# A DLRM tower on one core: a wait for the last group's landing ahead of each group of four gathers

## What is computed

```python
e = jnp.stack([tbl_0[ids[:, 0]], ..., tbl_26[ids[:, 26]]], axis=1)   # (2048, 27, 128)
dot = jnp.einsum('bnd,bmd->bnm', e, e)       # 27 x 27 products of each sample
z = dot.reshape(2048, 27 * 27)[:, idx]       # the 351 pairs i < j
h = jnp.concatenate([z, dense_ctx], axis=1)  # 367 features
h = jnp.maximum(h @ W_top1 + b_top1, 0.0)    # 512
h = jnp.maximum(h @ W_top2 + b_top2, 0.0)    # 256
y = h @ W_top3                               # (2048, 1)
```

## Time and profile before

| | us |
|---|---|
| time, median of 3 runs | 709.78 (707.19 to 711.47) |
| profiled execution, time | 705.33 |
| profiled execution, span from first to last instruction | 703.5 |
| TensorE matmuls busy | 407.6 |
| GpSimd busy | 246.3 |
| VectorE busy | 272.8 |
| ScalarE busy | 142.0 |

### The profile page before, as it was taken

How to read it: one execution, slowest core, us unless ns; L and a number is a source line. 1 busy time by engine, 2 the same in 40 slices (tenths; PEclk the granted TensorE clock), 3 DMA queues, 4 the chain that set the end, 5 groups by cost and what they waited for, 6 DMA issues and landing times.

```text
span 703.5 us, 15274 instructions
## 1 busy us (share of the span) xinstructions
PE 407.6 (58%) x6218; PEld 360.3 (51%) x6218; DVE 272.8 (39%) x804; ACT 142.0 (20%) x189; POOL 246.3 (35%) x264
## 2 busy tenths in 40 slices
PE   3327501892529724497245945179552892639875
PEld 3316401891429723396235935069441791529854
DVE  6506222781308603185032833028421581308211
ACT  3307210140103301023011321002210240103421
POOL 6750457007440347103561064600546007440000
PEclk9759755796759957599576976659766896759997
DMA  7921512011111211102111111110211111110000
GB/s 211 263 61 39 153 42 69 19 56 54 33 35 32 75 37 45 48 4 73 42 46 46 44 52 30 48 34 18 76 31 49 36 53 54 30 36 2 2 2 1
DMA packets 22295, 36.58 MB, mean 52 GB/s; under 512 B 12662, under 2 KB 13310, under 8 KB 22252
## 3 DMA queue, kind: packets, MB, share of 16 engines
q1 hardware_dynamic: 13996, 19.01, 9.3%
q0 software_dynamic: 8256, 16.92, 8.5%
HBM read 35.90 MB, written 0.01 MB: 51 GB/s over the span
## 4 chain that ended last, share of the span: by engine, by line
PE 52%; issue 32%; another core or an unknown queue 7%; DVE 3%; DMA 2%; ACT 2%; SPq 1%; DVEq 0%; ACTq 0%
PE emb_ps L670 20%; PE gram_ps L714 13%; PE mlp_ps L733 5%; PE emb_ps L706 4%; PE mlp_ps L747 3%; DMA embT<-in_tbl 2%; PE emb_ps L686 2%; DVE onehot L564 1%; PE mlp_ps L776 1%; PE mlp_ps L755 1%; PE mlp_ps L724 1%; SPq L271 1%; PE mlp_ps L781 1%; ACT onehot L425 0%
## 5 line engine op out<-in xcount | busy, mean ns | idle before, releaser
L391 POOL DMA_INDIRECT rows<-in_tbl,idx x256 | 244.0, 953 | 378.4 <-PE emb_ps L706 256.7
L714 PE MATMUL gram_ps<-embT 128*32 128x26 f32 x4096 | 97.0, 220 | 235.1 <-issue 214.6
L564 DVE TENSOR_SCALAR onehot<-ids_b,row_of 128x256 fp32r<-128x256 int32 x694 | 193.5, 356 | 44.9 <-PE emb_ps L670 37.5
L714 PEld LDWEIGHTS gram_ps<-embT 128*32 128x32 f32 x4096 | 74.1, 140 | 261.3 <-issue 240.0
L670 PE MATMUL emb_ps<-onehot,parts 125*128 125x256 f32 x1280 | 176.1, 298 | 48.0 <-issue 31.5
L670 PEld LDWEIGHTS emb_ps<-onehot,parts 125*128 125x128 f32 x1280 | 168.4, 203 | 52.3 <-issue 48.4
L576 DVE STREAM_TRANSPOSE turned<-gram_ps 128x832 f32<-128x832 f32 x16 | 16.8, 1050 | 309.4 <-PE gram_ps L714 284.8
L436 ACT ACTIVATE embT<-emb_ps 128x512 f32<-128x512 f32 x40 | 48.9, 1232 | 118.9 <-PE emb_ps L670 118.9
L444 ACT ACTIVATE embT<-emb_ps 128x512 f32<-128x512 f32 x32 | 36.4, 1237 | 167.4 <-PE emb_ps L706 141.3
L570 DVE COPY embT<-emb_ps 128x512 f32<-128x512 f32 x32 | 35.4, 1185 | 28.4 <-PE emb_ps L706 28.4
L733 PE MATMUL mlp_ps<-zT,w_sb 128*128 128x256 f32 (+1 forms) x168 | 38.7, 378 | 0.0
(11 more groups left out here) (43 smaller groups left out, 115.5 us busy)
## 6 DMA issues: line engine op xcount, KB each, us to landing
ids_b<-in_ids_mm SPq DMA_DIRECT2D x8, 896.0 KB
ids_b<-in_ids_mm SPq DMA_DIRECT2D x16, 256.0 KB
rows<-in_tbl,idx POOLq DMA_INDIRECT x256
embT<-in_tbl SPq DMA_DIRECT2D x6, 448.0 KB
w_sb<-in_tbl SPq DMA_DIRECT2D x2, 448.0 KB
turned<-in_tbl SPq DMA_DIRECT2D x1, 560.0 KB
w_sb<-in_W_top SPq DMA_DIRECT2D x1, 512.0 KB, 4.1
turned<-in_tbl SPq DMA_DIRECT2D x1, 448.0 KB
```

The costliest lines, as they stand in the source:

```text
L391: pool.indirect_dma_start(rows[:, t, n, :], None, tables[f], bass.IndirectOffsetOnAxis(idx[:, t, f:f + 1], 0), engine_sem=gathers_written) ...
L564: last = nc.vector.tensor_scalar(onehot[:, k % OH, c, :], ids_b[:, of, :], row_of[:, first + c:first + c + 1], None, ALU.is_equal)
L714: last = nc.tensor.matmul(gram_ps[q * COLS:(q + 1) * COLS, g * COLS:g * COLS + NJ], embT[:, t, at:at + COLS], embT[:, t, at:at + NJ], star ...
```

## The change

Ahead of each group of four gathers, after the wait for the transposes, GpSimd now also waits until the group that came last has landed: the group k - 1 of the same tile, or for k = 0 the last group of the other tile. In the first pair the first group of tile 0 has nothing to wait for.

```diff
@@ -385,6 +385,13 @@
 
                         past(pool, emb_filled, (p - 1) * JOBS + row_job(t, k) + 1)
                         pool.sem_inc(pool_waited, 1)
+
+                        if t or k:
+                            u, j = (t, k - 1) if k else (0, NT - 1)
+                            pool.wait_ge(s_rows[u][j], (p + 1) * 16 * len(TR[j]))
+                        else:
+                            past(pool, s_rows[1][NT - 1], p * 16 * len(TR[NT - 1]))
+                        pool.sem_inc(pool_waited, 1)
                         for n in TR[k]:
                             f = GATHERED[n]
                             one_queued((p * TILES + t) * NG + n + (TILES if first and t else extra))
```

## The result

The changed kernel took 573.2 us (median of 4 runs, 569.6 to 577.5), the kernel before 710.6 us beside it (4 runs, 707.2 to 712.7). The ratio is 0.807, 95% interval 0.801 to 0.814. The mechanism was rival A's, which had 14 in 100, with a time just above its 500 to 560.

What follows compares the result with a forecast made beforehand. The prediction took TensorE's grams, held beside GpSimd's gathers, to bound the kernel: 705.3 - 62 (14 grams shortened) + 7 (tile 1's later start) - 20 (pair 0) = 630 us, range 560 to 780.

Steps and rivals of the forecast that it cites:

- rival A: Pauses open wide: with a 1 us drain one or two pauses do for a gram; 500 to 540 us, 14 in 100.
- The link between gathers and TensorE: Gram matmuls creep beside gathers: 25.6 us instead of about 5; some 280 us in all hang on how gathers are spaced.
- rival C: No effect: TensorE's creeping is its own, 705 us, or pauses' cost and gain cancel; 5 in 100.
- The drain: Time until TensorE is free after a group's last write: a backlog growing with each gather, 1.3 to 1.8 us after four.
- the natural pause: GpSimd idle 1.72 us at 535.35 in the earlier trace: taken to buy about 22 matmuls and a shorter drain.
- The pause: On GpSimd, 3.15 us from a group's last gather start to the next group's first instead of 1.25, 1.9 more.
- The window: TensorE at full rate 0.4 to 0.9 us per pause; 65 gram matmuls each, gram over at about the third pause.
- the wait at k = 0: Ahead of a tile's first group: finds its group landed unless the short gram brings tile 1's turn early.
- Pair 0: Landing waits keep gathers apart, so the hold ending at 51.83 should mostly go: 20 of its 24 us gained.
- the cover up to 78.71: Pair 0's gathers end near 69 us, pair 1's start at 78.71 anyway: covered, about 9 us to spare.
- Tile 1's later start, +7,: Tile 1's gathers start about 1 us later than now in 7 pairs, adding 7 us.
- Rival B: Hold lasts through the pauses if the drain after four gathers exceeds about 2.2 us: 771 us, 33 in 100.

Runs made afterwards that it cites:

- experiment 1: The changed kernel with the landing wait only after each eight gathers instead of four: 683.7 us, ratio 0.965 to the kernel before.
- experiment 2: The changed kernel with the landing wait after each two gathers instead of four: 721.6 us, ratio 1.023 to the kernel before.
- experiment 3: The changed kernel with the wait met once three of a group's four gathers have landed: 666.5 us, ratio 0.936 to the kernel before.
- experiment 4: The kernel before, no landing waits; GpSimd runs four iotas ahead of each group of four gathers: 552.4 us, ratio 0.785.
- experiment 7: The kernel before with the change's landing waits in the first pair alone: 452.2 us against 430.4, on a chip without the hold.
- experiment 11: The kernel before, but all gathers of a pair wait for both grams of the pair before: 455.2 us against 430.2, ratio 1.063.
- experiment 5: The kernel before, no pauses; a tile's first gather waits for that tile's gram of the pair before: 421.9 us against 430.4, ratio 0.976.
- experiment 6: The kernel before with each gather replaced by a plain transfer and the lookup of gathered rows left out: 401.0 us against 430.4.
- experiment 8: The changed kernel with the landing wait only ahead of each run of 16 gathers: 443.6 us against 430.4, ratio 1.021.
- experiment 9: The changed kernel itself, unchanged, on a chip without the hold: 572.2 us against 432.9 for the kernel before, ratio 1.320.

## Why the prediction held, and where it didn't

**The link between gathers and TensorE: right, on these chips.** The gram's length is set by how gathers are spaced (experiments 1 to 4), and a stretch without writes is what frees it (4). The rule of the Trainium skill that the prediction weighed (SBUF — State Buffer, section "SBUF: two separate sides") agrees with the traces of two chips, where the grams beside gathers run as if alone (experiments 7 and 11: 3.78 us for 249 matmuls and 3.85 us for 256), and not with those of the others, where TensorE creeps only beside gathers. By that rule rival C's 705 should have stood; the profiled execution took 577.5.

**The drain: the step that failed.** "After 4 it should take less still, between 1.3 and 1.8." It took 0.95 us. The curve is 0.5 to 0.6 after 2, 0.95 after 4, 1.5 to 1.7 after 8, 3.0 after 16. The reading (more in a row, longer to drain) was right; the size after four was guessed from the natural pause after 7, which said "at most 1.85" and bounds nothing from below. That pause of 1.72 us was most likely too short to clear what the nine gathers before it had left: in experiment 1 seven gathers, behind a single one and a pause of 1.85 us, drain in 1.44 us.

**The pause.** 3.51 us from start to start, not 3.15: GpSimd is idle for 2.57 us from the end of its last write. That costs 2.26 us more than no pause, not 1.9.

**The window.** With an earlier start and a later end it was 2.0 us wide and passed 159 matmuls, not 65. So one or two pauses do for a gram, the grams take 4 to 14 us from their own start where the forecast had about 18 (21.2 from the first gather, which starts some 3 us ahead of the gram), and rival A's condition ("if the drain takes 1 us") was met.

**What became the bound.** The forecast held the wait at k = 0 for free and had three pauses a run. Since tile 1's gathers follow tile 0's at once, it is the fourth. Eight groups of 7.26 us are 58.1 us a pair; A had 55 to 60. In all GpSimd's stream takes 542.1 - 3.7 = 538.3 us: 64 groups, 464.6 less the last pause of 2.6, 462; two more gathers, 2.5; gathers that took far longer than 0.95 us, 39 ((1.104 - 0.953) x 256, with the mean of before's page); and 35 are left, nearly all of them for landings that took long: some 15 in pair 0 and some 20 in pairs 1 to 7, of which 11 in the four pauses beside the loads of ids. With 3.7 ahead, 33.6 behind and 1.8 around the span it is 577.5 us, the profiled execution. A's 500 to 540 lacked the 39 us, of which the trace of before showed nothing, and the 20, since the prediction took every landing of pairs 1 to 7 at 2.2 us.

**What was luck.** The forecast had the direction and the link, but the time came out in the range by two misses that pull apart: the windows passed far more than expected, which alone would have led to A's 500 to 540, outside the range, and the long gathers and landings, which the prediction hadn't counted, brought it back to 573.

**Pair 0: right in size, wrong in what covers it.** Its first gram starts at 58.5 instead of 74.4, 16 us sooner for a forecast of 20. Its gathers end at 79.3, not 69, as four waits for landings, not two, were long (5.1 to 7.9 us of idle time); the cover up to 78.71 was thus used up, and pair 1's first gather came 3.1 us later than before. On a chip without the hold the same gram starts at 50.6 in experiment 5, so the hold in pair 0 is worth some 24 us, as the earlier trace rows had it.

**Tile 1's later start, +7,** has no counterpart any more, since GpSimd no longer waits for TensorE there.

**Rival B** fell with the drain: 0.95 us is well under the 2.2 from which it decides. With the drain growing evenly from 1.6 us after 8 to 3.0 after 16, an estimate from these rows, a pause of 2.6 us would only fail behind runs of 13 or 14.

**What stays open.** What the hold is, and why some chips have it: the kernel before took 705, 708 and 711 us in three groups of runs and 430 to 433 in the three others, steady within a group. Whether plain transfers from GpSimd hold TensorE as well: experiment 6 met a chip without the hold. Nor do the runs show if the difference lies in the chip or in what else it was doing at that time; "a chip with the hold" is short for the chip of such a group. Nor where TensorE is held up: its instructions or its operands could come late, and no experiment separates the two.

## What to carry to other kernels

Where TensorE creeps beside gathers that GpSimd writes, space the gathers or keep them away from it; but price the spacing by the gathering engine's own stream (groups x pause) as soon as the hold is gone, since that becomes the bound at once. A wait for a landing is the dear way of making a gap. And try such a change on more than one chip: the same edit was 0.81 on one and 1.32 on another, while the variant without pauses gained on both.

## What the hardware showed unexpectedly

**The hold is there on some chips and not on others.** The kernel before: 705 to 711 us with TensorE held, mean granted clock 0.75 to 0.77, and 430 to 433 us without, at 0.93 to 0.96. The clock isn't what holds TensorE: in the earlier trace rows it creeps at 0.84 while gathers run, and passes 199 matmuls in 3.0 us at 0.53 once they are over.

**How the hold looks.** After some 40 matmuls that are taken up at once TensorE gets about five gram matmuls each 0.75 us behind a short run, and in a long run one instruction each 0.7 us, whatever the instruction (a gram matmul or a lookup).

**A gather behind a wait can be shut out by VectorE.** In the changed kernel:

```profile
102.66 16.46 DVE L571 TENSOR_SCALAR onehot<-ids_b,row_of 128x256 fp32r<-128x256 int32 x58
```

```profile
103.60 1.01 POOL L398 DMA_INDIRECT rows<-in_tbl,idx  x1 [2.48 <-DMA rows<-in_tbl,idx]
...
110.87 7.35 POOL L398 DMA_INDIRECT rows<-in_tbl,idx  x1 [2.51 <-DMA rows<-in_tbl,idx]
```

The second of these gathers takes 7.35 us while VectorE makes one-hots without a break. The Trainium skill (SBUF — State Buffer, section "SBUF: two separate sides") has it that VectorE in a mode that uses both port pairs locks GpSimd out, which then "cannot write the descriptors". No row shows which mode these one-hots run in. If it is that one, the trace agrees for this gather, 7.35 us for 0.95, but not for the first, 1.01 us at the start of the same run of one-hots, and not for one that follows another closely: in experiment 5

```profile
117.96 23.28 DVE L567 TENSOR_SCALAR onehot<-ids_b,row_of 128x256 fp32r<-128x256 int32 x74 [0.96 <-PE emb_ps L673]
```

```profile
118.70 0.94 POOL L394 DMA_INDIRECT rows<-in_tbl,idx  x1 [0.30 <-DMA rows<-in_tbl,idx]
...
139.92 0.95 POOL L394 DMA_INDIRECT rows<-in_tbl,idx  x1 [0.30 <-DMA rows<-in_tbl,idx]
```

the gathers from 118.70 to 139.92 take 0.94 to 0.95 us each beside an unbroken run of 74 one-hots. After pair 0, only gathers that come first behind a landing wait were shut out for 2 us or more (in the changed kernel and in experiments 2, 8 and 9), and not all of these: one at 244.87 in the changed kernel, 1.6 us into a run of one-hots, takes 0.94 us. None of those behind iotas in experiment 4 was. Why the pause makes the difference wasn't tried.
